# Score matmuls in half-column order: all first chunks, then all second chunks

## The reference, cut to what matters

```python
qn = _l2norm(q / scale)
kn = _l2norm(k / scale)
gv = beta[..., None] * v
nchunks = L // c                       # c = 64, L = 256
qc, kc, gvc = (to_chunks(qn), to_chunks(kn), to_chunks(gv))
attn = jnp.einsum('bnhid,bnhjd->bnhij', qc, kc)
...
mask = jnp.where(causal, decay, 0.0)
out = jnp.einsum('bnhij,bnhjd->bnhid', attn * mask, gvc)
```

## Time and profile before

| | |
|---|---|
| median of three runs | 2167.18 us (2166.52 to 2167.47) |
| profiled execution | 2164.84 us, its span 2163.1 us |
| TensorE busy with passes | 2135.4 us, 99% of the span |
| TensorE weight loads | 1752.6 us (overlap the passes) |
| VectorE, ScalarE, GpSimd | 1154.5, 1031.5, 522.2 us |
| granted TensorE clock | full speed over the whole span (1.00) |
| passes of the score line L866 | 2048, with 2048 loads |

### The profile page before, as it was taken

The page is one execution under the profiler, slowest core; times in us unless marked ns, Lnnn a source line. Parts: engine busy times, 40 slices in busy tenths (PEclk is TensorE's granted clock), DMA queues, the critical chain, the costliest instruction groups (busy, mean ns, idle before and its releaser), DMA issues.

```text
span 2163.1 us, 36173 instructions
## 1 busy us (share of the span) xinstructions
PE 2135.4 (99%) x12463; PEld 1752.6 (81%) x12463; DVE 1154.5 (53%) x2174; ACT 1031.5 (48%) x3300; POOL 522.2 (24%) x540
## 2 busy tenths in 40 slices
PE   8999999999999999999999999999999999999999
PEld 6778888888888887878888888888888888888887
DVE  6555654555555555555554445555555455545554
ACT  6655664665665665565565453333332333333232
POOL 2433443443443343343343441000000000000000
PEclk9999999999999999999999999999999999999999
DMA  8574443254355354354233221342334234323221
GB/s 264 185 239 133 146 138 123 81 162 139 93 145 159 84 154 136 95 147 142 106 143 113 70 107 49 129 170 98 127 125 149 88 121 156 103 97 113 96 94 63
DMA packets 191892, 274.79 MB, mean 127 GB/s; under 512 B 99184, under 2 KB 132960, under 8 KB 191712
## 3 DMA queue, kind: packets, MB, share of 16 engines
q1 hardware_dynamic: 191712, 272.49, 39.6%
HBM read 214.79 MB, written 57.67 MB: 126 GB/s over the span
## 4 chain that ended last, share of the span: by engine, by line
PE 92%; DVE 3%; ACT 2%; issue 2%; DMA 1%; DVEq 0%; POOL 0%; SPq 0%; ACTq 0%; POOLq 0%
PE proj_ps L651 49%; PE out_ps L651 14%; PE av_ps L877 5%; PE s_ps L866 4%; PE s_ps L924 3%; PE av_ps L924 3%; PE qt_ps L924 3%; PE kt_ps L924 3%; PE qt_ps L847 2%; PE kt_ps L852 2%; DMA head_scr<-stage 1%; PE misc_ps L670 1%; PE out_ps L721 0%; ACT squares L1117 0%; PE misc_ps L679 0%
## 5 line engine op out<-in xcount | busy, mean ns | idle before, releaser
L651 PE MATMUL proj_ps<-w_qkv,h_t 128*128 128x512 f32 x2304 | 618.0, 406 | 10.3 <-DVE q_sb L1428 2.1
L651 PEld LDWEIGHTS proj_ps<-w_qkv,h_t 128*128 128x128 f32 x2304 | 407.9, 188 | 103.3 <-issue 20.2
L651 PE MATMUL proj_ps<-h_t,w_qkv 128*128 128x512 f32 x1800 | 444.2, 391 | 0.3 <-issue 0.2
L651 PEld LDWEIGHTS proj_ps<-h_t,w_qkv 128*128 128x128 f32 x1800 | 335.6, 188 | 70.2 <-issue 1.3
L608 POOL TENSOR_TENSOR inv_norm<-guarded,minus_half 128x8 f32<-128x8 f32 x128 | 209.4, 1636 | 741.9 <-DVE guarded L1441 741.9
L1108 ACT ACTIVATE q_t<-qt_ps 128x512 f32<-128x512 f32 x128 | 76.3, 596 | 303.9 <-PE qt_ps L847 303.4
L651 PE MATMUL proj_ps<-h_t,w_gate 128*128 128x512 f32 x768 | 190.2, 398 | 2.6 <-ACT gate L1131 1.3
L1428 DVE TENSOR_TENSOR v_sb<-proj_ps,bias 128x512 f32<-128x512 f32 x128 | 88.5, 691 | 190.0 <-PE av_ps L877 183.4
L1117 ACT ACTIVATE squares<-q_sb 128x128 f32<-128x128 f32 x512 | 151.4, 297 | 56.9 <-DVE q_sb L1428 52.4
L1428 DVE TENSOR_TENSOR q_sb<-proj_ps,bias 128x512 f32<-128x512 f32 x128 | 88.4, 690 | 165.5 <-PE proj_ps L651 160.7
L651 PEld LDWEIGHTS proj_ps<-h_t,w_gate 128*128 128x128 f32 x768 | 139.8, 188 | 40.2 <-ACT gate L1131 10.7
(11 more groups left out here) (216 smaller groups left out, 3174.5 us busy)
## 6 DMA issues: line engine op xcount, KB each, us to landing
w_qkv<-tile_scr SPq DMA_DIRECT2D x100, 768.0 KB, 4.3
w_qkv<-head_scr SPq DMA_DIRECT2D x45, 1024.0 KB, 11.0
head_scr<-stage SPq DMA_DIRECT2D x30, 512.0 KB, 3.8
w_gate<-head_scr SPq DMA_DIRECT2D x15, 1024.0 KB, 4.9
w_out<-head_scr SPq DMA_DIRECT2D x15, 1024.0 KB, 4.9
tile_scr<-stage SPq DMA_DIRECT2D x25, 512.0 KB, 3.1
x_in<-_attn_hidden_states_dram SPq DMA_DIRECT2D x16, 512.0 KB, 6.7
h_scr<-stage SPq DMA_DIRECT2D x16, 512.0 KB, 3.3
```

Of the source, the lines that this page charges most:

```text
L651: mm = pe.matmul(out, w, y, start=(j == 0 and m == 0), stop=(3 * j + m == n - 1))
```

## The change

The two loops around the score matmul trade places. The eight matmuls, their operands, their outputs and the semaphore are the same; the order is chunk 0 of heads 0 to 3, then chunk 1 of heads 0 to 3, in place of chunk 0 and chunk 1 of head 0, then of head 1, and so on.

```diff
-                for h in range(HG):
-                    for c in range(P // CH):
+                for c in range(P // CH):
+                    for h in range(HG):
                         at = slice(h * P + c * CH, h * P + (c + 1) * CH)
                         mm = pe.matmul(s_ps[c * CH:(c + 1) * CH, at], k_t[:, at], q_t[:, at], start=True, stop=True)
                 mm.then_inc(scored, 1)
```

## The result

The changed kernel takes 2199.27 us (median of four, 2197.85 to 2200.28) against 2166.85 us for the kernel before in the same comparison: ratio 1.0152, 95% interval 1.0139 to 1.0166, so 30 to 36 us more. The forecast was 35.7 us more and a time of 2202.9 us. In a second comparison, with five runs, it was 2199.03 against 2165.36, ratio 1.0155 (1.0141 to 1.0169), 33.7 us.

A forecast was written before the change was run, and what follows sets the result against it. TensorE's order of work was taken as the bound; 0.279 us in each of 128 tiles gave 35.7 us, so 2200.5 from the profiled 2164.84, and 2202.9 with the median 2.3 higher; range 2190 to 2212, chance 0.78.

The forecast's parts named there:

- What bounds the kernel: Attention stage: TensorE busy 1252.7 of 1265 us, so a nanosecond added to its order of work is one of the kernel.
- The passing of B's instructions by A's waiting ones: Score burst: instructions for one column half are set aside while the other half's go past, handed out 1.7 ns each.
- strict order: Rival in the score burst: half A is done before B is looked at, 58.5 us, 2225.7 us; chance 0.08.
- The number of places: Score burst: six instructions set aside per column part, so B's first pass at 286 ns, 279 ns a tile; chance 0.60.
- seven: Rival, seven or eight places per part: B reached at A's fifth load or fourth pass, 27.9 us, 2195.1 us; chance 0.08.
- Five: Other reading of the boot burst, five instructions set aside per column part; inside the six-place forecast's own range, 2199 to 2206.
- The sum: Score bursts: 0.279 us longer in each of 128 tiles, 35.7 us in all.
- the few waits of TensorE for them could shrink by less than 1 us in all: TensorE's waits for the other engines, which get 0.28 us more per tile: less than 1 us back, left out.

The follow-up runs named there:

- The four regroupings: Four kernels reordering matmuls against the kernel before: three orders of the score matmuls, 2171.85, 2184.54 and 2184.54 us, and one of the start's modulation product, 2165.46 us.
- the pairs: Score matmuls ordered A A B B A A B B by column half, against the kernel before's A B A B A B A B: 2171.85 against 2165.71 us, ratio 1.0028.
- the triples: Score matmuls ordered A A A B B B A B by column half, against the kernel before: 2184.54 against 2165.71 us, ratio 1.0085.
- the switched order: Score matmuls ordered A B B B B A A A, the long run on half B, against the kernel before: 2184.54 against 2165.36 us, ratio 1.0089.
- the quarters: Kernel before with only the modulation product at the start regrouped, column quarter by quarter instead of in turn: one run, 2165.46 us.
- First chunks alone: Kernel before without the scores of every second chunk, half B's four matmuls, leaving 8 passes a tile: 2164.41 against 2165.71 us, ratio 0.9997.

## Why the prediction was right

**What bounds the kernel** was read rightly: nothing but TensorE's order changed, and the time follows the burst's length.

**The passing of B's instructions by A's waiting ones** is shown. B starts at 288 ns, ahead of A's sixth to eighth pass, which stand before it in the program. In strict order B's first pass would have come only with A's last, and the change would have cost 58.5 us. The Trainium skill (TensorE: Matmul & The Clock Gate, "Part 3: Packing small matmuls", "The mechanism") states that matmuls start and end in program order. The trace contradicts that between the halves, by the 288 ns; inside a half, order and distance hold.

**The number of places**, six, was an estimate from three instants of the sequencer. The prediction had B's first pass at 286 and the last at 743; they are at 288 and 744. The four regroupings put the stall where six places put it, on either half and on a quarter, and none fits seven. Five is excluded by the pairs alone. In the changed kernel, the triples, the switched order and the quarters a load of the full part starts 1 to 3 ns behind the pass that frees the sixth place, and five places would stall until that load. So the changed kernel's time would have come out the same with five; the choice of six was not tested by it. Whether six is a number of instructions or of three loads and three passes is open: in every burst here they alternate.

**One small pool for all parts** is a rival that neither the prediction nor the experiments name. By an estimate from the starts above, with seven places in all (the instruction just handed out takes one too) the score passes of every order tried start within some 6 ns of where they do with six places for each half; with eight or more B would start well ahead of 288. The semaphore instruction excludes it. The same 44 instructions stand ahead of that instruction before and after. Before, it comes at 44 ns, when two loads and two passes have started (the next two loads are seen between 642.990 and 643.080), so such a pool would have handed out eleven at most, and eleven would have been enough. After, eleven would be handed out once A's second pass has started, at 107 ns, and the instruction would come soon behind that; it comes at 304. With six places for each part, sixteen are handed out without a stall before, and only at 284 ns after.

**The sum** was 35.7 us in the bursts; they grew by 35.9. The time grew by 32.4 and 33.7, so 2.2 to 3.5 us are missing. The step that was mis-sized is "the few waits of TensorE for them could shrink by less than 1 us in all". By the stretches of the attention stage, TensorE was idle for 1265 - 1252.7 = 12.3 us before, and is for 10.5 us in the longer stage after:

```profile
60.00:1362.00 1302.00, 1291.51 (x8379) 1064.55 (x8378) 693.84 (x1394) 726.84 (x2729) 499.82 (x509) 1.00 0.41 126
```

That is 1.8 us in place of "less than 1". Two more traces bear it out: in that of the quarters, whose attention stage is the kernel before's, the idle time is 13.2 us, and in the second one of the changed kernel 10.6. So 1.7 to 2.7 us came back. The edited line says the same from first start to last: before, 1322.9 - 41.1 = 1281.8 us, in the trace of the quarters 1282.5; after, 1315.8 in both traces. That is 33.3 to 34.0 us for 35.9 of longer bursts. The rows are those of the quarters and of the changed kernel's second trace:

```profile
L866 PE MATMUL s_ps<-q_t,k_t x2048: 222/222/271, 41.0 to 1323.5; 128*64 128x64 f32 x187
```

```profile
L866 PE MATMUL s_ps<-q_t,k_t x2048: 222/222/272, 41.0 to 1356.8; 128*64 128x64 f32 x187
```

The prediction looked at the longest entry in the list of what the passes wait for, 1.7 us, and not at the list's sum. The entries that the list shows add up to 7.3 us before and 5.0 after (7.4 and 5.2 in the two other traces). Among the waits for other engines the one that shrinks most in both comparisons is that for VectorE's bias add of Q, to free a bank, before (60 to 1325 us) and after (60 to 1362):

```profile
PE proj_ps L651 <- DVE q_sb L1428: 1.0, 2, 0.6
```

```profile
PE proj_ps L651 <- DVE q_sb L1428: 0.3, 1, 0.3
```

It is 1.1 in the trace of the quarters and 0.3 in the changed kernel's second. One such place, the V projection behind a burst, before and after:

```profile
271.56 0.47 PE L651 MATMUL proj_ps<-w_qkv,h_t 128*128 128x512 f32 x1 [0.58 <-DVE q_sb L1428]
```

```profile
275.78 0.47 PE L651 MATMUL proj_ps<-w_qkv,h_t 128*128 128x512 f32 x1 [0.28 <-DVE q_sb L1428]
```

The burst in front is 0.28 us longer and the wait 0.30 shorter: in that tile the change cost nothing. The rest of what came back is spread over small waits and not accounted for one by one.

Of the 2.9 us between the bursts' 35.9 and the first trace's 33.0, 1.9 to 2.0 lie in that stretch, 0.2 behind the last burst, and 0.8 ahead of the first one, which starts at 41.1 us before and 40.3 after; in the second trace of the changed kernel it starts at 41.0, so this was chance. For the other orders the intervals, 2 to 3 us to either side, are too wide to say what came back: by the medians nothing with the pairs (6.1 in the bursts, 6.1 in the time), 2.2 us with the triples and 2.7 with the switched order.

No order tried beats head by head. First chunks alone show why: eight passes of one half took 457 ns by themselves, and the order before ends at 464.

## What to carry to other kernels

Matmuls that use different parts of the array's columns ran side by side from start to end only where the program dealt them out in turn. Count the instructions that one part gets in a row: with two passes per fp32 matmul each is four instructions; one matmul at a time cost nothing, runs of two cost 47 ns a burst, a run of four 280. When TensorE is the bound, add up its whole list of waits, and not the longest entry, before calling its idle time nothing.

## What the runs showed of the hardware that was not expected

A part of the columns accepts six instructions that haven't started (shown for a half by the pairs; a quarter fits six and, by its passes alone, five), and one full part stops the handing out for all.

Half of the passes can cost nothing: 1024 score passes left out changed the time by a ratio of 0.9997 (0.9988 to 1.0006).

The instant at which the sequencer passes a semaphore instruction is a gauge of TensorE's queue: 22, 44, 265, 194, 304 and 957 ns after the first loads of six different bursts fit one queue of 28 and one delay of 18 ns. Both are estimates; no row shows either by itself.

A half that starts from idle has its first two passes 107 ns apart and the others 58, A at 0 and 107, B after the change at 288 and 394; a late start costs the first gap again, though it lies beside the other half's passes.
